# Eight of ten blocks' sums placed by node, and a third near tile in every run of a graph network's layers

## The reference, cut to what matters

```python
def _gine_layer(x, src, dst, edge_attr, eps, We, be, W1, b1, gamma, beta, W2, b2):
    e = edge_attr @ We + be
    m = jax.nn.relu(x[src] + e)
    agg = jax.ops.segment_sum(m, dst, num_segments=x.shape[0])
    h = ((1.0 + eps) * x + agg) @ W1 + b1
    mu = jnp.mean(h, axis=0)
    var = jnp.mean(jnp.square(h - mu), axis=0)
    h = (h - mu) * jax.lax.rsqrt(var + BN_EPS) * gamma + beta
    h = jax.nn.relu(h)
    return jax.nn.relu(h @ W2 + b2)
for l in range(L):          # L = 4
    x = _gine_layer(x, src, dst, edge_attr, eps[l], We[l], be[l], W1[l], b1[l], gamma[l], beta[l], W2[l], b2[l])
return _layernorm(x0 + x, axis=-1)
```

## Time and profile before

| what | value |
|---|---|
| median of 3 runs | 1289.77 us |
| time of the profiled execution | 1291.98 us |
| its span | 1290.2 us |
| its mean granted TensorE clock | 0.965 |
| TensorE busy (matmul) | 1206.8 us, 94% |
| VectorE busy | 1035.1 us, 80% |
| GpSimd busy | 783.0 us, 61% |
| ScalarE busy | 553.4 us, 43% |
| moved by DMA | 254.22 MB, mean 197 GB/s |
| chain that ended last, by engine | GpSimd 42%, TensorE 29%, issue 15%, VectorE 11% |

### The profile page before, as it was taken

The page is one execution under the profiler, slowest core; times in us unless marked ns, Lnnn a source line. Parts: engine busy times, 40 slices in busy tenths (PEclk is TensorE's granted clock), DMA queues, the critical chain, the costliest instruction groups (busy, mean ns, idle before and its releaser), DMA issues.

```text
span 1290.2 us, 26518 instructions
## 1 busy us (share of the span) xinstructions
PE 1206.8 (94%) x7483; PEld 769.3 (60%) x7483; DVE 1035.1 (80%) x2134; ACT 553.4 (43%) x1159; POOL 783.0 (61%) x831
## 2 busy tenths in 40 slices
PE   2878999999999999999998999999998999999997
PEld 2874566666655566656655566666644566666653
DVE  7988878888866978877776978887767888788768
ACT  1923444444374444434364443434345434443333
POOL 0055677677606777777706777777714777777720
PEclk9558999999999999999998999999989999999999
DMA  3167677667736777777746777777746777777753
GB/s 113 56 189 213 193 207 217 198 203 217 223 104 209 217 217 217 217 217 217 239 132 198 217 216 217 217 217 218 239 127 189 216 217 216 217 217 217 221 179 113
DMA packets 92577, 254.22 MB, mean 197 GB/s; under 512 B 19902, under 2 KB 23114, under 8 KB 92428
## 3 DMA queue, kind: packets, MB, share of 16 engines
q0 software_dynamic: 65600, 215.01, 57.1%
q1 hardware_dynamic: 25804, 36.42, 8.7%
q10 hardware_dynamic: 1024, 1.05, 0.3%
HBM read 239.24 MB, written 12.97 MB: 195 GB/s over the span
## 4 chain that ended last, share of the span: by engine, by line
POOL 42%; PE 29%; issue 15%; DVE 11%; DMA 2%; ACT 1%; ACTq 0%; POOLq 0%; DVEq 0%
POOL rows L827 42%; PE y_ps L2106 10%; PE y_ps L1985 6%; PE pair_ps L1932 4%; DVE rows L1543 3%; DVE rows L1429 2%; PE h_ps L2063 1%; PE y_ps L2117 1%; DMA rows<-node_table,src_fast 1%; PE h_ps L1858 1%; DVE src_onehot L1360 1%; PE uT_ps L2016 1%; DMA node_table<-rows 1%; PE pair_ps L2049 1%; PE uT_ps L2023 1%
## 5 line engine op out<-in xcount | busy, mean ns | idle before, releaser
L827 POOL DMA_INDIRECT rows<-node_table,src_fast x820 | 780.4, 952 | 452.8 <-issue 248.3
L1543 DVE SCALAR_TENSOR_TENSOR rows<-We_ps,negw_fast,rows 128x512 f32<-128x512 f32 x820 | 565.4, 742 | 85.4 <-DMA rows<-node_table,src_fast 84.5
L1985 PE MATMUL y_ps<-table_parts,src_onehot 128*128 128x512 f32 x1664 | 430.9, 410 | 21.8 <-DMA src_onehot<-near_ws 8.5
L1985 PEld LDWEIGHTS y_ps<-table_parts,src_onehot 128*128 128x128 f32 x1664 | 292.6, 191 | 191.8 <-issue 94.3
L1003 ACT ACTIVATE rows<-y_ps 128x512 f32<-128x512 f32 x416 | 248.7, 598 | 217.6 <-PE y_ps L1985 210.8
L1932 PE MATMUL pair_ps<-rows,onehot 128*32 128x512 f32 x2504 | 306.7, 602 | 13.7 <-DVE rows L1543 13.5
L1360 DVE TENSOR_TENSOR src_onehot<-y_ps,src_bc 126x256 fp32r<-126x256 f32 x376 | 149.6, 414 | 60.9 <-PE y_ps L1985 60.4
L1932 PEld LDWEIGHTS pair_ps<-rows,onehot 128*32 128x32 f32 x2504 | 67.9, 109 | 150.5 <-issue 111.8
L2063 PEld LDWEIGHTS h_ps<-uT,W_sb 128*128 128x128 f32 x1152 | 133.8, 192 | 6.0 <-issue 3.3
L2063 PE MATMUL h_ps<-uT,W_sb 128*128 128x128 f32 x1152 | 134.7, 275 | 2.9 <-issue 2.9
L2106 PE MATMUL y_ps<-rows,hT 128*128 128x512 f32 x288 | 124.5, 593 | 0.0
(11 more groups left out here) (251 smaller groups left out, 793.9 us busy)
## 6 DMA issues: line engine op xcount, KB each, us to landing
late_rows<-node_table SPq DMA_DIRECT2D x1536, 2.0 KB
rows<-node_table,src_fast POOLq DMA_INDIRECT x820
b_bc<-node_table ACTq DMA_DIRECT2D x512, 2.0 KB
node_table<-rows SPq DMA_DIRECT2D x29, 256.0 KB, 3.7
src_onehot<-near_ws SPq DMA_DIRECT2D x416, 2.0 KB
x_now<-x_pad SPq DMA_DIRECT2D x10, 512.0 KB, 7.6
W_sb<-W SPq DMA_DIRECT2D x4, 1024.0 KB, 5.5
rows<-W SPq DMA_DIRECT2D x16, 256.0 KB
```

The lines of the kernel that those rows point to most:

```text
L827: nc.gpsimd.indirect_dma_start(rows[:, slot, :], None, table[:, :], bass.IndirectOffsetOnAxis(src_fast[:, t:t + 1], 0)).then_inc(landed[q] ...
L1543: last = nc.vector.scalar_tensor_tensor(rows[:, slot, :], We_ps[:, :], negw_fast[:, t:t + 1], row, ALU.mult, ALU.max)
L1985: last = nc.tensor.matmul(y_ps[k % 2][:, :], src_onehot[:, 2 * (k % ONEHOTS) + b, :], table_parts[:, part, 2 * pair_of(k) + b, :], start=( ...
```

## The change

The third tile of the runs that had two goes to TensorE as well: `EXTRA_RUNS` covers them all, `TWO_RUNS` is gone. There are 108 near tiles a layer, 12 in each of the first nine steps, and 20 extra lanes, of which nine are still made ahead on ScalarE. Blocks 0 to 7 (`BY_NODE`) are placed by node: the matrices `place` are the stationary operand, 32 columns at a time, and the halves and the carry stream through, so that the sums stand in PSUM by node, not transposed (`place_block`, after the second group). VectorE adds them to u (`add_sums`, after the messages of the fourth group), and TensorE turns the whole (`turn_block`, after its fourth group and before the batch of near tiles). Blocks 8 and 9 are placed as before; in the last step the products with W1 stand after the third group instead of the second. Two small LayerNorm tiles move into `stats`.

```diff
+    BY_NODE = BLOCKS - 2
-    EXTRA_RUNS = [slice(LONG_A_STEP + 1, LONG_RUNS, LONG_A_STEP), slice(2 * LONG_A_STEP + 3, LONG_RUNS, 2 * LONG_A_STEP)]
-    TWO_RUNS = slice(LONG_A_STEP + 3, LONG_RUNS, 2 * LONG_A_STEP)
+    EXTRA_RUNS = [slice(LONG_A_STEP + 1, LONG_RUNS, LONG_A_STEP), slice(LONG_A_STEP + 3, LONG_RUNS, LONG_A_STEP)]
...
-        ln_stats = sb("ln_stats", [P, BLOCKS, 6])
-        ln_mv = sb("ln_mv", [P, BLOCKS, 2])
+        ln_stats = stats[:, 0, 0:BLOCKS, :]
+        ln_mv = stats[:, 1, 0:BLOCKS, 0:2]
...
+        node_sums = turned_uT
...
-                    (TWO_RUNS, slice(2, 6), first[:, rest_lanes(TWO_RUNS), :]),
-                    (TWO_RUNS, slice(6, 8), last[:, rest_lanes(TWO_RUNS), :]),
...
             def scale_u(n, i):
 
-                if n:
-                    act.wait_ge(u_turned, n)
+                if i == BLOCKS - 1:
+                    act.wait_ge(u_turned, n // BLOCKS * (BLOCKS - BY_NODE) + i - BY_NODE)
+                elif n:
+                    act.wait_ge(block_summed, n + 1)
...
+            def add_sums(n, l, i):
+
+                dve.wait_ge(u_ready, n + 1)
+                dve.wait_ge(block_placed, BY_NODE * l + i + 1)
+                nc.vector.tensor_tensor(u[:, :], node_sums, u[:, :], ALU.add).then_inc(u_whole, 1)
...
-                        if q == (3 if i < BLOCKS - 1 else 1) and l == 0:
+                        if q == (3 if i < BLOCKS - 1 else 2) and l == 0:
                             keep_w(i).then_inc(w_sum_ready, 1)
...
+                        if q == 3 and 0 < i <= BY_NODE:
+                            add_sums(n - 1, l, i - 1)
...
                     sum_quad(q, l, i)
+                    if q == 3 and 0 < i and not final:
+                        turn_block(n - 1, l, i - 1)
...
                     if 0 < i:
-                        if q == (0 if final else 1):
+                        if final and q == 0:
                             open_block(n - 1, l, i - 1, True)
                             add_first_pair(n - 1, l, i - 1)
-                        if q == 1:
+                        if final and q == 1:
                             close_block(n - 1, i - 1)
-                        if q == (1 if final else 3):
+                        if not final and q == 1:
+                            place_block(n - 1, l, i - 1)
+                        if q == (2 if final else 3):
                             product_h(n - 1, l, i - 1)
...
+            def place_block(n, l, i):
+
+                pe.wait_ge(uT_copied, n + 1)
+                pe.wait_ge(place_ready, n + 1)
+                pe.wait_ge(pair_copied[0], n + 2)
+                pe.wait_ge(pair_copied[1], n + 2)
+                if i:
+                    pe.wait_ge(carry_copied, (BLOCKS - 1) * l + i + 1)
+                nodes = [slice(g * WIN, (g + 1) * WIN) for g in range(P // WIN)]
+                for g in range(PLACED // WIN):
+                    nc.tensor.matmul(node_sums[nodes[g], :], place0(i)[:, nodes[g]], pair_sb[:, 0, :],
+                                     start=True, stop=g == 1 or g == 0 and not i)
+                nc.tensor.matmul(node_sums[nodes[3], :], place1(i, WIN, 2 * WIN), pair_sb[:, 1, :], start=True, stop=True)
+                if i:
+                    nc.tensor.matmul(node_sums[nodes[0], :], place1(i - 1, HALF, PLACED), carry[:, :],
+                                     start=False, stop=True)
+                nc.tensor.matmul(node_sums[nodes[2], :], place1(i, 0, WIN), pair_sb[:, 1, :],
+                                 start=False, stop=True).then_inc(block_placed, 1)
+
+            def turn_block(n, l, i):
+
+                pe.wait_ge(u_whole, BY_NODE * l + i + 1)
+                for c in range(C):
+                    last = nc.tensor.matmul(uT_ps[:, c, :], u[:, c * P:(c + 1) * P], ident[:, :],
+                                            start=(c == 0), stop=True, is_transpose=True, skip_group_check=True)
+                last.then_inc(block_summed, 1)
```

More of the change, by code:

```diff
@@ L477, in gnn_layers @@
         u_turned = sem("u_turned")
+        block_placed = sem("block_placed")
+        u_whole = sem("u_whole")
         u_ready = sem("u_ready")
```

## The result

The changed kernel takes 1324.12 us in the median (1323.04 to 1325.49); the kernel before takes 1289.6 beside it. The ratio is 1.0251, with a 95% interval of 1.0227 to 1.0275, that is 32 us; the two medians lie 34.5 us apart. The profiled execution takes 1324.6 us with a span of 1322.8, against 1291.98 and 1290.2 before. The forecast was 1316, 1303 to 1328.

The account below looks back on a forecast made before the run. SP's queue, 2.33 us a near tile, was taken to bound layers 1 to 3. Layer 0 with preparations +10.9, then +6.1, +4.2, +5.1: together +26.3 on a 1290.2 us span, giving 1316.5, median 1316, range 1303 to 1328.

Parts of the forecast that it names:

- the likeliest case: Whole kernel: SP's queue paces layers 1 to 3; 1316 us, between 1309 and 1322, chance 64 in 100.
- signs of being wrong: Near_ws waits vanish, first near tile comes near 106, or layer 0 alone grows by over 20 us.
- Layers 1, 2 and 3: SP's longer loop starts the last near tile 7.95 us later; less saved waits, +6.1, +4.2 and +5.1 us.
- Rival one: Gathers on GpSimd bound the kernel and SP's rows arrive in time: -15 us, 1275 us; chance 9 in 100.
- The preparations: Before layer 0's first near tile: four more extra lanes at 2.98 us each, +11.9 us.
- Rival three: Preparations: four extra lanes' products run at full clock, +6.4 instead of +11.9 us, 1311 us; chance 10 in 100.
- TensorE's step: Twelve near tiles a step: placing saves 1.2 us, a later relu adds 1.15; 25.9 us, under SP's 27.9.
- The relu: First relu of a step's gathered tiles on ScalarE comes later, so the third tile waits: 1.15 us a step.
- the wait ahead of W1: Last step of each layer: W1 products move behind the third group, covering a wait, -0.7 us a layer.
- Layer 0: Preparations and layer 0 together: SP's late last tile gives +11.6, less 0.7 in the last step, +10.9 us.
- Its own chain: TensorE's own work in layer 0, preparations included: +9.2 us, so SP decides by 2 us.
- Rival two: Placing and its waits cost 1.6 us a step; TensorE's chain decides layer 0, +22, 1326 us; chance 12 in 100.

Follow-up runs that it names:

- after_sp8: Changed kernel with SP's late rows in pieces of eight at every second loop turn instead of four at every turn: 1303.57 us, ratio 1.0078.
- after_relu: Changed kernel with ScalarE's relus of the first four groups ahead of its copies of carry, u and first pair: 1318.65 us, ratio 1.0201.
- after_wide: Changed kernel with two idle 512-column products added on TensorE behind each late extra lane: 1328.37 us, ratio 1.0271.
- after_ahead12: Changed kernel with twelve instead of nine extra lanes made ahead on ScalarE: 1317.72 us, ratio 1.0206.
- best108: Changed kernel with eight-row SP pieces, earlier relus, ScalarE's late-row loads behind the weights' copies, and twelve lanes ahead: 1274.15 us, ratio 0.9844.
- tiles_only: Kernel before with the four more tiles a layer and twenty extra lanes, old placing kept: 1318.94 us, ratio 1.0189.
- after_act: Changed kernel with two of ScalarE's late-row loads a step moved behind the copies of the weights' pair: 1314.67 us, ratio 1.0175.
- place_only: Changed kernel with the old 104 tiles a layer and sixteen extra lanes, so only the placing by node is new: 1298.77 us, ratio 1.0037.

## Why the prediction was right, and where it was off

The sign and the main cause were right: the likeliest case, SP's queue as the pace of layers 1 to 3. The 1324 us measured lie inside the range of 1303 to 1328, but above the 1309 to 1322 of the likeliest case, and one of the prediction's own signs of being wrong came true: layer 0 alone, with the preparations, grew by over 20 us. Its steps, one by one.

**SP.** Tile 106 was to leave SP at 341.7 in layer 0; it left at 341.73. That closeness is luck in part. Nothing in the prediction lets SP's loop start otherwise than with TensorE's first near tile; this came 14.9 us later, but tile 10 left SP at 118.75, only 11.5 us later than in the earlier trace rows, because two waits for DMAs ahead of it took 1.2 us instead of 4.5. Layers 1, 2 and 3 were to grow by 6.1, 4.2 and 5.1 us; from first to last group they grew by 5.5, 4.1 and 4.8. The turn stayed at 2.32 us (429.33 to 652.30 for 96 turns). GpSimd waits for TensorE late in each layer (8.7, 7.8 and 9.4 us), and TensorE not at all for gathered rows in a layer's last 20 us, as foretold. Rival one is out by the same rows, and after_sp8 and after_relu show it by experiment.

**The preparations, +11.9 predicted, +14.9 measured.** The price of a lane was right, 2.98 us. The step that failed is the one that added four lanes to a start which it left as it was: the seven lanes of the earlier trace rows take 17.95 us, and seven times 2.98 are 20.9. The missing 2.9 us are the window at 0.93 in the earlier trace rows, which stood in the rows on which I built, and I took it as given. In the changed kernel it is gone. Whether the change is the reason is not shown, and more speaks against it. With nine lanes ahead all six profiled kernels with 108 tiles lack it (after_wide, where TensorE's work differs, has it), and all three with 104 tiles have it. But after_ahead12 and best108 have the same preparations, and one has granted clocks of 0.80 and 0.63 from 76 to 84 us, the other 0.50 in both windows; their first tiles are 3.3 us apart. So it can come and go with nothing changed ahead of it. What all fourteen traces share is an earlier sign: the point at which the clock fell near 36 us, long before the late lanes, while TensorE was almost idle. From 34 to 38 us the granted clock averages 0.72 to 0.80 in the eight that lack the later stretch, and 0.62 to 0.67 or 0.83 to 0.92 in the six that have it. Windows of the kernel before and of the changed one:

```profile
34.00:38.00 4.00, 0.03 (x1) 0.06 (x1) 3.57 (x4) 3.97 (x11) 0.00 (x0) 0.67 0.18 54
```

```profile
34.00:38.00 4.00, 0.00 (x0) 0.00 (x0) 3.41 (x4) 3.97 (x11) 0.00 (x0) 0.74 0.15 44
```

This is an agreement among single executions, not an experiment. If it holds, the 2.9 us belong to the execution and not to the change.

**Rival three** is out: at 0.50 the four lanes cost what the earlier trace rows said. The Trainium skill (TensorE: Matmul & The Clock Gate, What's actually happening) lets the clock follow how busy TensorE has been; the trace does not agree, with 154 products in an unbroken 33.01 us at 0.50, and after_wide changed nothing in that from 80 us on. The same section of the Trainium skill says that what the gate looks at runs freely and isn't tied to the kernel, so that the point of a change varies; with that, a stretch of full clock that after_ahead12 has and best108 has not (same preparations) agrees. What would hold the clock up here wasn't found.

**TensorE's step.** Six products were to cost 1.71 us. From the placing's start at 832.15 to the turning at 835.69 in layer 2 it is 3.54 us; less 1.85 for the two groups between them, that is 1.69. (The 0.14 us of drain in the 1.71 stand in no row that the prediction names.) The second round of products ran beside the next group's sums. The relu was to come late by 1.15 us; it was 1.04. The step was to be 25.9 us; after_sp8 shows 25.88. In the last step the wait ahead of W1 is gone: from its first group to its last it is 15.9 us, 16.5 in tiles_only.

**Layer 0, +10.9 predicted with the preparations, +22.9 measured.** This is the second step that failed, in three parts. The 2.9 us above are one. The second is a wait that the sum put at nothing without naming it: the prediction followed ScalarE from the copy of uT on, but not what it does ahead of the copies for the weights' placing, which TensorE reaches earlier by just what it saves. The wait for pair_w is 9.2 us in nine steps, and after_act gives 9.5 back. These two are the 12.0 us that were missing. The third part moved nothing in the sum but was wrong in kind: SP was said to decide layer 0, by 2 us, with tile 107 on TensorE at 345.6. In fact TensorE came to tile 106 14.9 us behind its issue. Its own chain was to give +9.2 and gave, without the lost clock and the placing, about +11.5 (tiles_only: the layer's last group 14.4 us later, less 2.9), as much as I had taken from SP. That the two agree is luck: the chain that decided was the other one. Behind the preparations the four tiles alone cost layer 0 nothing.

Rival two had the size (layer 0 +22, and 1326 us is nearer to the 1324 measured than the forecast's 1316), but not the cause: there was no third round of placing, and no wait for VectorE that counts. The step was 1.0 us longer than without the placing because of two waits for ScalarE.

**What was not in the sum** and helped: -4.2 us between the layers, where the granted clock was higher (1.00, 0.97, 1.00 instead of 0.97, 0.94, 0.97). The prediction had only named the stretch at the end of layer 2 as one that may go. It named the waits for gathered rows that end with the change, but took from them only their own length.

Errors by part: +3.0 in the preparations, +9.2 in layer 0 behind them (8.2 against -1.0), -0.6, -0.1 and -0.3 in layers 1 to 3, -4.2 between them, -0.6 at the ends. They add up to +6.4, and the forecast of the span was 6.3 low. The rest up to the 8 us between the medians is the difference of a single execution to the median (2.2 us in the kernel before, 0.5 in the changed one).

## What to carry to other kernels

Where several queues run level, taking work from one of them only helps if what it is moved to has slack in every queue that feeds it: here a tile taken from the gathers (1.25 us) put one more turn on a queue that only issues DMAs (2.33 us). Find that out by taking instructions out of the suspected queue in both kernels: it gave the changed one 1.7% and the one before nothing. And when a piece of work on the bounding engine gets shorter, look up for the very next instruction when each of its inputs is ready; if that instruction belongs to only one stage, its wait is in no other stage's rows.

## What the runs showed of the hardware that I had not expected

A queue that issues DMAs can pace a kernel while it is never "busy" on the page: four row loads with places from registers, one index load and one fixed DMA take 2.33 us on SP; with two turns' eight rows behind one index load it is 4.15 us for the two. Six products on four column groups and the eight of the next two groups of sums take 3.54 us together, 0.25 each, with no gap between the kinds of work. TensorE stayed at a granted clock of 0.50 for 33 us of unbroken two-column products, and from 80 us on also with 512-column products every 3.7 us between them (after_wide), while a short stretch at full clock came in some traces and not in others at the same place. Between the layers the same products took 154.4 us in the changed kernel, where the granted clock was 1.00, 0.97 and 1.00, and 161.0 us in place_only, where it was 0.97, 0.87 and 1.00.
